# Transposing attention probabilities through the full TensorE array instead of through its halves

## The chip, the cores and the metric

The kernel runs on one core of one Trainium2 chip, as one program. The metric is the device time of one execution in microseconds. The core has a matrix engine (TensorE, PE in the profile, its weight loads PEld), VectorE (DVE), ScalarE (ACT), GpSimd (POOL) and SyncE (SP), which issues the DMA transfers. Each engine works through its own list of instructions in order; they meet through semaphores. All results of TensorE go to PSUM, which has eight banks here, each of 128 partitions by 512 numbers of 4 bytes.

## The reference

Two layers over a batch of 32 graphs of 512 nodes with 512 features, all in float32. The second layer is attention with 8 heads of 64 features, masked by the adjacency matrix:

```python
# layer 0
y = einsum('nm,bmd->bnd', adj, x)
x = layernorm(x + einsum('bnd,do->bno', y, weight) + bias)
# layer 1
qkv = (x @ w_qkv).reshape(b, n, 3, H, hd).transpose(2, 0, 3, 1, 4)
attn = einsum('bhnd,bhmd->bhnm', q, k) * hd ** -0.5
attn = where(adj == 0, -inf, attn)
attn = softmax(attn, axis=-1)
o = einsum('bhnm,bhmd->bhnd', attn, v).transpose(0, 2, 1, 3).reshape(b, n, d)
o = o @ w_proj + b_proj
out = layernorm(x + o + (layernorm of o with gamma and beta))
```

## The kernel before, in words

Every matrix product is made of three products of float32r operands: a number is split into a rounded part (hi) and the rest (lo), and hi*hi, hi*lo and lo*hi are added in PSUM. ScalarE makes the hi part by a copy, VectorE (for one tensor GpSimd) the lo part by a subtraction.

**The first layer** (0 to about 800 us) runs over the batch in rounds: `y` (line 332) and `z` (line 345) are matmuls over the full array, 128 rows by 512 columns. Between them, once a round, `turn_two` (line 221) transposes the previous result by halves of the array. Before the first round the adjacency is transposed once, by 16 transposes over the full array (line 152).

**The second layer** (the rest) goes through the batch `b`, and in each through 16 steps `k`: 4 pairs of heads (`group = k // 4`) by 4 blocks of 128 query rows (`k % 4`). A step has a chain that runs over all engines, spread over several steps:

- TensorE, `scores(b, k)` (line 819): scores of both heads of the pair for 128 query rows, 512 keys. One head has 64 features, so each matmul uses 64 rows of the array, and the two heads sit in its upper and lower half and run side by side, into two banks `s_bank`.
- VectorE, `masked_max` (line 1239), ScalarE, `exponent` (line 1119), VectorE, `inverse` (line 1248), GpSimd, `normalise` (lines 718 and 721): the softmax. The result is `probs[:, k % 2, a, :]`, for head `a`, with 128 query rows on the partitions.
- TensorE, `turn(k)` (line 835): transposes of `probs`, so that the keys come onto the partitions, into two banks `t_bank`. It signals `probs_turned`. In the profile this operation is named `bank<-ident,probs`: the probabilities are the weights, and the identity is what moves.
- ScalarE, `pt_hi_part` (line 1126), and VectorE, `pt_lo_part` (line 1259): the two parts of the transposed probabilities, out of `t_bank` into `pt_hi` and `pt_lo`. The views `turned` and `turned_into` say which part of a bank goes where.
- TensorE, `attend_v` (line 858): when the four query blocks of a pair are there, probabilities times values, again in two halves of the array (64 keys each).

Between these, TensorE is given filling work: the projections for values, queries and keys of the next batch, and the output projection (`half_pair`, lines 870 and 872, for the last batch also line 959). All of it is written as pairs of 64-row matmuls in the two halves of the array. The order on TensorE is written out by hand, in `first_step`, `second_step`, `third_step` and `last_step`: each begins with `turn(k)`, then come filling work or `attend_v`, then `scores` for step `k + 3`, and then the next turn. `ready_to_turn` holds TensorE before a turn until the probabilities are normalised and the lo part of the turn before has been taken from `t_bank`. The wait in `inverse` holds VectorE until a turn has read `probs`, because the next scores' maximum writes the same buffer.

SyncE loads and stores rows of whole batches and is not touched by the change.

Of the kernel before, what the change touches and what calls it, by code (L numbers as in the profile page):

```python
# [13 lines left out]
P = 128  # L14
# [4 lines left out]
def graph_layers(nc, x, adj, w0, b0, wqkv, wproj, bproj, gamma, beta, out):  # L19
    B, N, D = x.shape  # L20
    T = N // P
    HEAD = 64
# [16 lines left out]
    with ExitStack() as whole:  # L39
# [11 lines left out]
        ident = whole.enter_context(nc.sbuf_tensor("ident", [P, P], F32, side="right"))  # L51
# [21 lines left out]
        with ExitStack() as first:  # L73
            def sb(name, shape, dt):
                return first.enter_context(nc.sbuf_tensor(name, shape, dt))

            def sem(name):
                return whole.enter_context(nc.semaphore(name))
# [293 lines left out]
            def _(act):  # L372
# [33 lines left out]
                def batch(b, first=False, last=False):  # L406
                    for j in range(T):
                        y_hi_part(b, j)
                        w_hi_part(b, j)
                        if not first and j == 1:  # L410
                            for turned in range(T):
                                ut_hi_part(b - 1, turned)
                    if not last:
                        x_hi_part(b + 1)
                    if not first:
                        act.wait_ge(ub_made, b * 4)
                        act.wait_ge(u_turned, b * 4)
                    normalise(b, 0)
                    w_hi_part(b, 4)
                    normalise(b, 1)  # L420
                    w_hi_part(b, 5)
                    normalise(b, 2)
                    w_hi_part(b, 6)
                    normalise(b, 3)
                    w_hi_part(b, 7)
# [12 lines left out]
            def _(dve):  # L438
# [49 lines left out]
                def batch(b, first=False, last=False):  # L488
                    for j in range(T):
                        y_lo_part(b, j)  # L490
                        w_lo_part(b, j)
                        if not first and j == 1:
                            for turned in range(T):
                                ut_lo_part(b - 1, turned)
                    if not last:
                        x_lo_part(b + 1, 0)
                        x_lo_part(b + 1, 1)
                    row_stats(b, 0, free=not first)
                    if not last:
                        x_lo_part(b + 1, 2)  # L500
                    row_shift(b, 0)
                    row_stats(b, 1, free=not first)
                    if not last:
                        x_lo_part(b + 1, 3)
                    row_shift(b, 1)
                    w_lo_part(b, 4)
                    row_stats(b, 2)
                    row_shift(b, 2)
                    w_lo_part(b, 5)
                    row_stats(b, 3)  # L510
                    row_shift(b, 3)
                    w_lo_part(b, 6)
                    w_lo_part(b, 7)
# [13 lines left out]
        with ExitStack() as second:  # L527
# [11 lines left out]
            probs = sb("probs", [P, 2, 2, N], F32)  # L539
# [20 lines left out]
            s_bank, t_bank, o_bank = psum[0:2], psum[2:4], psum[4:6]  # L560
            g_bank = psum[6:8] + o_bank
            TOP, BOTTOM = slice(0, HEAD), slice(HEAD, P)
# [16 lines left out]
            probs_turned = sem("probs_turned")  # L579
# [41 lines left out]
            assert max(S_STEP) <= max(R_STEP) < 2 * STEPS  # L621

            def turned(i):
                return t_bank[i][:].rearrange("p (a m n) -> p a m n", a=2, m=T)

            def turned_into(rows, k, i):
                first = k % T * P + i * HEAD
                return rows[:, :, :, first:first + HEAD]

            def rows_of(b, n):  # L630

# [172 lines left out]
            def _(pe):  # L804
# [24 lines left out]
                def turn(k):  # L829

                    for a in range(2):
                        for m in range(T):
                            for i, h in enumerate((TOP, BOTTOM)):
                                cols = slice((a * T + m) * HEAD, (a * T + m + 1) * HEAD)
                                last = pe.transpose(t_bank[i][:, cols], probs[h, k % 2, a, m * P:(m + 1) * P],  # L835
                                                    ident[h, h])
                                if a == 1 and m == T - 1:
                                    last.then_inc(probs_turned, 1)

                def attend_v(b, p, part, run, half=None):  # L840

# [123 lines left out]
                def last_pair(b):  # L965

                    done = 4 * B - 4
                    turn(13)
                    pe.wait_ge(o_made, done)
                    pe.wait_ge(otlo_made, done + 2)  # L970
                    last_project(0, 0, (0, 1), first=True)
                    ready_to_turn(b, 14)
                    pe.wait_ge(proj_half, done + 2)
                    last_project(0, 1, (0, 1))
                    turn(14)

                    pe.wait_ge(ot_summed, b * 8 + 2 * LAST)
                    outputs(b, 0)
                    ready_to_turn(b, 15)
                    turn(15)  # L980
                    pe.wait_ge(otlo_made, done + 3)
                    last_project(0, 1, (2,))
# [132 lines left out]
            def _(act):  # L1115
# [5 lines left out]
                                       accum_out=sums[:, k % 4, a:a + 1]).then_inc(exp_made, 1)  # L1121

                def pt_hi_part(b, k):
                    act.wait_ge(probs_turned, b * 32 + (2 * k + 2))
                    for i in range(2):
                        act.activation(turned_into(pt_hi, k, i), turned(i), ACT.Copy).then_inc(pthi_made, 1)  # L1126

                def qk_hi_part(b, i):
# [52 lines left out]
                def batch(b, last_part=True, more=True):  # L1181
                    for k in range(STEPS):
                        group, part = divmod(k, T)
                        if part == 3 and group == 1:

                            ot_hi_part(b, 0)
                        if k == STEPS - 1 and not more:
                            last_ot_halves(0)
                        pt_hi_part(b, k)
                        if k == STEPS - 1 and not more:  # L1190
                            last_ot_hi(0)
                        if k + 2 < STEPS or more:
                            exponent(b, k + 2)
                        if part == 0 and (last_part or group > 0):
                            ot_halves(*pair_before(b, group))
                        if part in (1, 2):
                            unit_hi(b, k, 2 * part - 2, more)
                            unit_hi(b, k, 2 * part - 1, more)
                        if part == 1 and group != 1 and (last_part or group > 0):
                            ot_hi_part(*pair_before(b, group))  # L1200
                        for n in rows_at(k, Z_STEP) if last_part else ():
                            scaled(b, n)
                        for batch_row in rows_done(b, k, R_STEP, last_part):
                            result(*batch_row)
# [29 lines left out]
            def _(dve):  # L1234
# [18 lines left out]
                def pt_lo_part(b, k):  # L1253
                    if k % T == 0 and not (isinstance(b, int) and b * STEPS + k == 0):

                        dve.wait_ge(pv_done, b * 8 + k // 2)
                    for i in range(2):
                        dve.wait_ge(pthi_made, b * 32 + (2 * k + i + 1))
                        dve.tensor_tensor(turned_into(pt_lo, k, i), turned(i), f32(turned_into(pt_hi, k, i)),  # L1259
                                          ALU.subtract).then_inc(ptlo_made, 1)  # L1260
# [182 lines left out]
```

## Time and profile before

| | us |
|---|---|
| median of 3 runs | 3365.83 (3362.24 to 3365.88) |
| profiled execution, its own time | 3366.38 |
| its span in the trace | 3364.6 |
| TensorE busy, matmuls | 3308.5 (98%) |
| TensorE weight loads | 2923.1 (87%) |
| VectorE busy | 2623.7 (78%) |
| ScalarE busy | 2229.6 (66%) |
| GpSimd busy | 1997.1 (59%) |

The busy time of an engine is the time in which at least one of its instructions runs; matmuls overlap, since the end of one lies behind the start of the next, so the rate of TensorE is read from the distance between starts and not from durations. The transposes of line 835 are 8192 of TensorE's 31792 matmul records. The first layer is the part with heavy DMA traffic (168 to 195 GB/s in the slices that lie wholly in it), the second layer has 27 to 70 GB/s. The granted clock of TensorE is 1.0 or near it in all slices, with 0.8 in the first and the last.

### The profile page before, as it was taken

How to read it: one execution, taken by the hardware profiler on the slowest of the kernel's cores; microseconds unless marked ns; L12 is line 12 of the kernel's file. 1: busy time of each engine (PE TensorE's matmuls, PEld its weight loads, DVE VectorE, ACT ScalarE, POOL GpSimd, SP SyncE). 2: the span in 40 equal slices, each digit the busy share in tenths (PEclk: the TensorE clock that was granted, in tenths of full speed). 3: DMA queues.
4: the chain of work that ended last, by engine and by line, in shares of the span. 5: the costliest groups of instructions: out<-in, count | busy, mean ns of one | idle time of the engine just before them, and what ended most of it. 6: DMA issues, size and time to landing. Idle time of an engine off the chain costs nothing. (4 is left out here: it accounts for less than half of the span.)

```text
span 3364.6 us, 88016 instructions
## 1 busy us (share of the span) xinstructions
PE 3308.5 (98%) x31792; PEld 2923.1 (87%) x31792; DVE 2623.7 (78%) x6434; ACT 2229.6 (66%) x4634; POOL 1997.1 (59%) x2690
## 2 busy tenths in 40 slices
PE   8999999998999999999999999999999999999996
PEld 6888888886899998889899899899999899998894
DVE  7666666665788888888888888888888888888887
ACT  4444444444677777777777777777777777777775
POOL 4555556552466666666666666666666666666666
PEclk8999999998999999999999999999999999999998
DMA  5565555653011111111122211111111111111210
GB/s 188 174 195 168 186 187 172 190 180 102 27 52 51 55 54 51 51 55 51 51 63 66 66 51 51 51 51 51 51 54 54 51 51 54 51 51 53 70 59 32
DMA packets 345217, 279.62 MB, mean 83 GB/s; under 512 B 13713, under 2 KB 275857, under 8 KB 344977
## 3 DMA queue, kind: packets, MB, share of 16 engines
q1 hardware_dynamic: 344976, 275.83, 27.0%
q8 instruction: 222, 3.64, 0.5%
q14 instruction: 19, 0.15, 0.0%
HBM read 141.56 MB, written 134.22 MB: 82 GB/s over the span
## 5 line engine op out<-in xcount | busy, mean ns | idle before, releaser
L1126 ACT ACTIVATE pt_hi<-bank 128x512 fp32r<-128x512 f32 x1024 | 557.0, 596 | 546.3 <-PE bank L835 533.9
L1119 ACT ACTIVATE probs<-probs,bias_row 128x512 f32<-128x512 f32 x1024 | 731.7, 721 | 44.7 <-DVE bias_row L1239 43.6
L1259 DVE TENSOR_TENSOR pt_lo<-bank,pt_hi 128x512 fp32r<-128x512 f32 x1024 | 658.0, 684 | 44.0 <-PE bank L858 34.3
L721 POOL TENSOR_SCALAR probs<-probs,inv_sums 128x480 f32<-128x480 f32 (+1 forms) x1024 | 685.3, 682 | 0.0
L1239 DVE CUSTOM_DVE_ANT_0 probs<-bank,mask_bias 128x512 f32<-128x512 f32 x1024 | 661.9, 684 | 9.7 <-PE bank L819 5.8
L718 POOL TENSOR_TENSOR probs<-probs,inv_sums 128x32 f32<-128x32 f32 x512 | 122.7, 240 | 730.4 <-DVE inv_sums L1248 730.3
L872 PE MATMUL bank<-x_lo,w_hi 64*128 64x512 f32 x1024 | 403.3, 394 | 0.0
L870 PE MATMUL bank<-x_lo,w_hi 64*128 64x512 f32 x1024 | 403.3, 394 | 0.0
L872 PE MATMUL bank<-x_hi,w_hi 64*128 64x512 f32 x992 | 403.2, 406 | 0.0
L870 PE MATMUL bank<-x_hi,w_hi 64*128 64x512 f32 x992 | 401.6, 405 | 0.0
L835 PEld LDWEIGHTS bank<-ident,probs 64*128 64x128 f32 x8192 | 362.9, 139 | 40.8 <-issue 4.9
L870 PE MATMUL bank<-x_hi,w_lo 64*128 64x512 f32 x992 | 385.6, 389 | 0.0
L872 PE MATMUL bank<-x_hi,w_lo 64*128 64x512 f32 x992 | 385.3, 388 | 0.0
L835 PE MATMUL bank<-ident,probs 64*128 64x64 f32 x8192 | 350.6, 222 | 2.9 <-DVE pt_lo L1259 2.9
L1248 DVE RECIPROCAL inv_sums<-sums 128x2 f32<-128x2 f32 x512 | 84.0, 164 | 291.4 <-PE bank L835 287.5
L384 ACT ACTIVATE u<-res,shift,rstd 128x512 f32<-128x512 f32 x128 | 104.7, 818 | 307.0 <-DVE shift L467 307.0
L858 PE MATMUL bank<-pt_hi,v 64*128 64x512 f32 (+1 forms) x2064 | 299.3, 403 | 4.2 <-ACT pt_hi L1126 3.9
L858 PE MATMUL bank<-pt_lo,v 64*128 64x512 f32 (+1 forms) x2064 | 297.0, 399 | 0.4
L300 POOL TENSOR_TENSOR rstd<-var_eps,half_neg 128x1 f32<-128x1 f32 x128 | 95.8, 748 | 338.2 <-DVE var_eps L462 338.2
L761 POOL TENSOR_TENSOR ot_lo<-ot,ot_hi 128x512 fp32r<-128x512 f32 x127 | 164.5, 1295 | 209.3 <-ACT ot_hi L1161 209.3
L858 PEld LDWEIGHTS bank<-pt_hi,v 64*128 64x128 f32 x2064 | 208.3, 187 | 49.3 <-issue 32.1
L819 PE MATMUL bank<-k_hi,q_hi 64*128 64x512 f32 x1024 | 215.5, 390 | 8.0 <-DVE bias_row L1239 8.0
(139 smaller groups left out, 10847.2 us busy)
## 6 DMA issues: line engine op xcount, KB each, us to landing
x_in<-in_x_dram SPq DMA_DIRECT2D x32, 1024.0 KB, 5.2
u_beta_rows<-ub SPq DMA_DIRECT2D x32, 1024.0 KB, 4.4
ut_hi<-ut_hi_sb SPq DMA_DIRECT2D x128, 256.0 KB, 4.1
ut_lo<-ut_lo_sb SPq DMA_DIRECT2D x128, 256.0 KB, 3.8
x_lo<-ut_lo SPq DMA_DIRECT2D x128, 256.0 KB, 4.7
out_dram<-o SPq DMA_DIRECT2D x128, 256.0 KB, 3.2
ub_row<-u_beta_rows SPq DMA_DIRECT2D x124, 256.0 KB, 2.7
x_hi<-ut_hi SPq DMA_DIRECT2D x124, 256.0 KB, 4.4
```

Of the source, the lines that this page charges most:

```text
L718: pool.tensor_tensor(probs[:, k % 2, 0, strip], probs[:, k % 2, 0, strip], inv_sums[:, k % 4, 0:1].to_broadcast((P, STRIP)), ALU.mult)
L721: pool.tensor_scalar(probs[:, k % 2, a, cols], probs[:, k % 2, a, cols], inv_sums[:, k % 4, a:a + 1], 0.0, ALU.mult, ALU.add)\
L761: pool.tensor_tensor(ot_lo[:, p, :], ot[:], f32(ot_hi[:, p, :]), ALU.subtract)\
L819: last = pe.matmul(s_bank[a][:], l[h, pair, n * P:(n + 1) * P], r[h, pair, :], start=i == 0, stop=i == 2)
L835: last = pe.transpose(t_bank[i][:, cols], probs[h, k % 2, a, m * P:(m + 1) * P], ident[h, h])
L858: last = pe.matmul(bank[a][:, cols], w, part[h, a, m, cols], start=first and m == 0, stop=end and m == T - 1)
L870: top = pe.matmul(banks[run][:], left[run][TOP], right[run][TOP], start=run == 0 and first, stop=run == 1 and end)
L872: bottom = pe.matmul(banks[1 - run][:], left[1 - run][BOTTOM], right[1 - run][BOTTOM], start=run == 0 and first, stop=run == 1 and end)
L1119: act.activation(probs[:, k % 2, a, :], probs[:, k % 2, a, :], ACT.Exp, bias=bias_row[:, k % 4, a:a + 1], scale=-1.0, accum_out=sums[:, k ...
L1126: act.activation(turned_into(pt_hi, k, i), turned(i), ACT.Copy).then_inc(pthi_made, 1)
L1239: dve.tensor_tensor_reduce(probs[:, k % 2, a, :], s_bank[a][:], mask_bias[:, k % T, :], -SCALE, 3.0e38, ALU.add, ALU.min, bias_row[:, k % ...
L1259: dve.tensor_tensor(turned_into(pt_lo, k, i), turned(i), f32(turned_into(pt_hi, k, i)), ALU.subtract).then_inc(ptlo_made, 1)
```

## The change

`turn(k)` transposes 128 query rows by 128 keys at a time over the full array, with the whole identity, where it took 64 query rows by 128 keys in one half of the array and the other 64 rows in the other half. There are 8 transposes a step in place of 16. Before, bank `i` of `t_bank` held query rows `64 i` to `64 i + 63` of both heads; now bank `a` holds all 128 query rows of head `a`. `probs_turned` still rises by two a step, now once when head 0 is through and once when head 1 is. The views `turned` and `turned_into` follow the new layout, and ScalarE waits before each of its two copies for that head's signal, where it waited once for both. `pt_hi` and `pt_lo` hold the same numbers in the same places as before. Nothing else changes, and the order of the parts on each engine stays as it is.

```diff
             def turned(i):
-                return t_bank[i][:].rearrange("p (a m n) -> p a m n", a=2, m=T)
+                return t_bank[i][:].rearrange("p (m n) -> p m n", m=T)
 
             def turned_into(rows, k, i):
-                first = k % T * P + i * HEAD
-                return rows[:, :, :, first:first + HEAD]
+                return rows[:, i, :, k % T * P:(k % T + 1) * P]
...
                     for a in range(2):
                         for m in range(T):
-                            for i, h in enumerate((TOP, BOTTOM)):
-                                cols = slice((a * T + m) * HEAD, (a * T + m + 1) * HEAD)
-                                last = pe.transpose(t_bank[i][:, cols], probs[h, k % 2, a, m * P:(m + 1) * P],
-                                                    ident[h, h])
-                                if a == 1 and m == T - 1:
-                                    last.then_inc(probs_turned, 1)
+                            cols = slice(m * P, (m + 1) * P)
+                            last = pe.transpose(t_bank[a][:, cols], probs[:, k % 2, a, cols], ident[:])
+                            if m == T - 1:
+                                last.then_inc(probs_turned, 1)
...
                 def pt_hi_part(b, k):
-                    act.wait_ge(probs_turned, b * 32 + (2 * k + 2))
                     for i in range(2):
+                        act.wait_ge(probs_turned, b * 32 + (2 * k + i + 1))
                         act.activation(turned_into(pt_hi, k, i), turned(i), ACT.Copy).then_inc(pthi_made, 1)
```

## Rows read from the trace of the kernel before

**Rows 1.** The page's first part: busy us, share of span, instructions.
```profile
PE 3308.5 (98%) x31792; PEld 2923.1 (87%) x31792; DVE 2623.7 (78%) x6434; ACT 2229.6 (66%) x4634; POOL 1997.1 (59%) x2690
```

**Rows 2.** Stretches: length, busy PE, PEld, DVE, ACT, POOL, granted clock, DMA share, GB/s.
```profile
100.00:770.00 670.00, 667.86 (x3698) 548.50 (x3694) 444.08 (x924) 279.08 (x460) 374.12 (x345) 1.00 0.59 183
870.00:3200.00 2330.00, 2329.97 (x25396) 2117.67 (x25393) 1922.41 (x4926) 1748.92 (x3760) 1443.29 (x2110) 1.00 0.19 54
```

**Rows 3.** What TensorE waited for, whole run: total us, times, longest.
```profile
PE bank L819 <- DVE bias_row L1239: 8.0, 5, 2.1
...
PE bank L858 <- ACT pt_hi L1126: 3.9, 3, 1.3
...
PE bank L835 <- DVE pt_lo L1259: 2.9, 3, 1.0
```

**Rows 4.** TensorE in time order around one turn: start us, length us, instruction.
```profile
2002.84 0.42 PE L819 MATMUL bank<-k_hi,q_hi 64*128 64x512 f32 x2
...
2003.29 0.42 PE L819 MATMUL bank<-k_hi,q_lo 64*128 64x512 f32 x2
2003.53 0.68 PE L835 MATMUL bank<-ident,probs 64*128 64x64 f32 x16
2003.99 0.47 PE L870 MATMUL bank<-w_hi,ot_hi 64*128 64x512 f32 x1
...
2004.31 0.38 PE L870 MATMUL bank<-w_lo,ot_hi 64*128 64x512 f32 x1
```

**Rows 5.** Line 835: the page's group; then weight loads in attention, min/median/max ns.
```profile
L835 PE MATMUL bank<-ident,probs 64*128 64x64 f32 x8192 | 350.6, 222 | 2.9 <-DVE pt_lo L1259 2.9
...
L835 PEld LDWEIGHTS bank<-ident,probs x7957: 134/139/221, 869.9 to 3333.0; 64*128 64x128 f32 x199
```

**Rows 6.** Full-array transposes of line 152: durations, and single ones in time order.
```profile
L152 PEld LDWEIGHTS bank<-ident,u x16: 141/230/231, 3.5 to 6.9; 128*128 128x128 f32 x16
L152 PE MATMUL bank<-ident,u x16: 273/421/476, 3.5 to 7.0; 128*128 128x128 f32 x16
...
4.61 0.63 PE L152 MATMUL bank<-ident,u 128*128 128x128 f32 x2
...
6.94 0.38 PE L152 MATMUL bank<-ident,u 128*128 128x128 f32 x2
...
7.05 0.27 PE L152 MATMUL bank<-ident,u 128*128 128x128 f32 x1
```

**Rows 7.** Busy time and granted clock (third number from the end) in the first stretches.
```profile
3.00:5.00 2.00, 1.49 (x7) 1.52 (x8) 0.85 (x2) 0.00 (x0) 0.00 (x0) 1.00 0.93 274
...
12.00:16.00 4.00, 3.31 (x8) 2.64 (x9) 4.00 (x5) 2.72 (x6) 2.79 (x2) 0.50 1.12 343
18.00:24.00 6.00, 6.00 (x28) 4.92 (x28) 4.89 (x7) 2.77 (x6) 1.84 (x2) 1.00 0.60 195
```

**Rows 8.** Full-array matmuls of 512 columns at both clocks, in time order.
```profile
14.56 1.91 PE L332 MATMUL bank<-adjt_lo,x_hi 128*128 128x512 f32 x4
...
21.25 1.07 PE L332 MATMUL bank<-adjt_lo,x_hi 128*128 128x512 f32 x4
```

**Rows 9.** Half-array transposes between full-array matmuls, first layer; matmuls, then weight loads.
```profile
422.95 0.39 PE L332 MATMUL bank<-adjt_hi,x_lo 128*128 128x512 f32 x1
423.27 1.21 PE L221 MATMUL bank<-ident,u 64*128 64x64 f32 x32
424.41 0.50 PE L332 MATMUL bank<-adjt_hi,x_hi 128*128 128x512 f32 x1
...
424.74 0.40 PE L332 MATMUL bank<-adjt_hi,x_hi 128*128 128x512 f32 x1
...
423.27 1.07 PEld L221 LDWEIGHTS bank<-ident,u 64*128 64x128 f32 x32 [0.35 <-issue]
```

**Rows 10.** The page's costliest groups: ScalarE's copy and VectorE's subtraction of the transposed probabilities.
```profile
L1126 ACT ACTIVATE pt_hi<-bank 128x512 fp32r<-128x512 f32 x1024 | 557.0, 596 | 546.3 <-PE bank L835 533.9
...
L1259 DVE TENSOR_TENSOR pt_lo<-bank,pt_hi 128x512 fp32r<-128x512 f32 x1024 | 658.0, 684 | 44.0 <-PE bank L858 34.3
```

## The prediction, made before the changed kernel ran

> **What bounds the kernel now.** I read the busy times first, then a table of the stretches, then who waited for whom, then the order of time around one step. TensorE is busy for 98% of the span [rows 1]. In the long stretch of attention, 870 to 3200 us, it is busy for 2329.97 of 2330 us at a granted clock of 1.00, while VectorE has 1922, ScalarE 1749 and GpSimd 1443 us [rows 2]. Busy alone could hide stalls, so the waits: on the lines of attention TensorE waited for another engine 8.0, 3.9 and 2.9 us in the whole run (lines 819, 858 and 835), 14.8 us together [rows 3]. The two halves of the array run side by side, and the start of one pair of 64-row matmuls comes 0.23 us after the start of the pair before (2002.84 and 2003.29, with one more pair between them) [rows 4]. So the end is set by how long the TensorE stream is, and a change of the transposes is worth what it does to that stream, nearly one to one. The ScalarE waits for transposes and the idle time of VectorE and GpSimd cost nothing now.
>
> **What a turn costs before.** There are 512 turns (32 batches of 16 steps), 8192 transposes [rows 5]. The last score pair starts at 2003.29, so it is through its slot at 2003.52; the turn starts at 2003.53 and the next work starts at 2003.99; but that first pair is long (0.47 where others take 0.39) and the second one starts at 2004.31, 0.32 later, not 0.23 [rows 4]. From slot end to the regular rhythm again: 2004.31 - 0.23 - 2003.52 = **0.56 us** a turn. Of this the transposes are 16 in two streams: 0.68 less one duration of 0.22 over 15 intervals is 0.031 us each, 0.061 a pair, 0.49 for eight pairs; 0.07 is the way back to matmuls with long weights.
>
> **What a turn costs after.** Removed: 16 transposes of 64 rows by 64 moving columns, two at a time. Added: 8 transposes of 128 rows by 128 moving columns, one at a time. Work by columns: before 8 pairs of 64, after 8 of 128, so if a column costs the same, the streaming doubles.
>
> The trace of before has this very operation, on the adjacency at the start (line 152, 128*128 by 128x128, the same data type): the last two start at 6.94 and 7.05, **0.11 us** apart, and last 0.27 us, the smallest duration [rows 6]. The earlier ones last 0.42 and are 0.21 apart (two that start at 4.61 are through after 0.63) [rows 6]. Which is the one to use? The granted clock is recorded as 1.00 from 3 to 5 us and as 0.50 from 12 to 16 us [rows 7], but the factor of two with the same shape is that between the two levels of the clock: the 128x512 matmuls of line 332 take 1.91 us for four at 14.56, where 0.50 was granted, and 1.07 at 21.25, with 1.00 [rows 7, 8]. I take 0.11, the only value that fits the full level, and keep 0.21 as the upper end. The lower end is 0.061, the interval of a pair of half-array transposes, if the load of the 128 weight columns and not the moving columns sets it: 8 x 0.11 = 0.88 (0.49 to 1.68).
>
> **The change between halves and full array.** All else in attention is 64-row work, so each turn now goes over to the full array and back. That also is in the trace, with the parts exchanged: in the first layer 32 half-array transposes stand between full-array matmuls. The last full matmul before starts at 422.95, its slot of 0.23 ends at 423.18; the transposes start only at 423.27; the first full matmul after starts at 424.41, takes 0.50 in place of 0.39, and the second follows at 424.74 [rows 9]. From slot end to rhythm: 424.74 - 0.23 - 423.18 = 1.33 us. Sixteen pairs at 0.061 are 0.98, so the round trip costs **0.35 us**: 0.09 in which TensorE stands before the transposes, about 0.05 for a first weight load with nothing over it, 0.09 and 0.11 for the same on the way back. The weight loads show it too: an idle time of 0.35 us ended by issue, where otherwise a load runs under each matmul [rows 9]. The Trainium skill, TensorEngine Tiling (Array Packing), Key Properties, says that changing the tiling mode drains TensorE, which the gap before 423.27 agrees with.
>
> A turn after is thus 0.88 + 0.35 = 1.23 us, against 0.56. The 0.07 of the way back before is replaced by the round trip's own. **Difference 0.67 us x 512 = +343 us.**
>
> **What hides or gives back.** Nothing lies over it: TensorE is the engine with no gaps. The way of a step that runs beside it (turn done, reciprocal and scores' maximum, the low part, next turn) starts from the end of a turn and has the same TensorE work as before to run under, so it isn't late now. The waits that exist (14.8 us) can shrink, since ScalarE gets its first tile when four transposes are through and no longer after all 16, and the long weights' exposure adds room; I take 4 us back of them. The new wait on ScalarE, one for each tile, sits ahead of the copies of line 1126, where ScalarE waits for TensorE already (533.9 us of idle time in all), so what is queued behind it (exponents, values' copies) comes no later relative to the end of the turn. The copies of 1126 and the subtractions of 1259 now read and write blocks of 128 and not 64 elements; 512 elements a row as before, at 596 and 684 ns [rows 10]; if each changed by a tenth, it would be in the shade of TensorE. The queue of SyncE is untouched. The last turn starts at 3333.0 [rows 5], so the last 32 us, where the layer norms of the last rows end the program, have none.
>
> Sum against the profiled execution: 3366.4 us (its span 3364.6), + 343 - 4 = 3705. The median of the runs shown is 3365.83, the same within 0.02%. **Forecast 3705 us**, +10%.
>
> **Rivals.**
> - The way there and back costs nothing here, because the neighbours are 64-row matmuls, whose drain might lie under the other half. For: nothing in rows 4 shows such a cost when transposes follow matmuls in one mode. Against: rows 9 at both edges, in the same form in all later rounds of the first layer. Turn 0.88 + 0.07 = 0.95, +0.39 x 512 = +200: 3566 us.
> - The moving columns of a full transpose are not the limit, the weight load is (0.061 each). For: a weight load of 64 rows and one of 128 rows take the same (139 ns, the median of line 835, and 141 ns, the smallest of line 152) [rows 5, 6], so eight loads in place of sixteen would be no more work. Against: the 0.11 at 6.94 to 7.05. Turn 0.49 + 0.35 = 0.84, +143: 3509 us. The skill's TensorE page (TensorE: Matmul & The Clock Gate, Back-to-back issue gap) gives some 81 ns for a sustained pair of load and 128-column matmul; by it the turn would be 1.00 us and the time about 3590. The row disagrees with 81 ns, and is for this data type; the chance of this rival covers that value too.
> - **Faster, the other side**: the transposes are bound by their number, 0.031 us for each issued whatever its size. Then eight cost 0.25, and with no cost of changing over the turn is 0.32: -0.24 x 512 = -123, 3243 us. This is what would make the edit a gain. It decides at (0.56 - change-over) / 8: a full transpose would have to take under 0.06 us with a free change-over, under 0.03 with the one measured. Against it stands again the 0.11.
> - TensorE falls to its lower clock level in places, because it now stands still twice in each step and spends more on transposes. If one step in ten ran at half clock, attention (about 2840 us after) would add some 280: near 3990 us. For: in a stretch in which TensorE was busy 3.31 of 4.00 us, 0.50 was granted [rows 7]. Against: 100 to 770 us, with such round trips, has 1.00 throughout [rows 2]. The skill's section PE-mode transpose says that transposes do not count as busy for the clock in the way matmuls do; the stretch with 32 of them in each round does not show a fall.
> - 0.21 us a full transpose at full clock: turn 2.03, +753: 4119 us.
>
> **How the numbers follow.** Forecast 0.84; free change-over 0.05; weight-load bound 0.04; faster by number of instructions 0.02; fallen clock 0.03; 0.21 us each 0.01; 0.01 for something that leaves the time alone. The range needs only the forecast's own uncertainty: the interval of a full transpose is read at 0.01 us (0.105 to 0.115 is 0.04 a turn, 20 us in all), the round trip may differ from 0.35 by 0.05 with halves as neighbours (26 us), the waits by 10 us: 3650 to 3755. A measurement of this kernel tells about 0.2% (7 us) from no change: faster 0.02, same 0.01, slower 0.97.
>
> **What will show it.** In the profile after: 4096 transposes of 128*128 128x128, median 0.27 us long, starting 0.11 apart (the main term; at 0.06 the second rival holds); the first one some 0.09 us later than the slot end of the last score pair, and the pair after the turn long, about 0.50 (else the first rival); 1.23 us from slot end to rhythm; granted clock 1.00 in the long stretch; TensorE still without waits in it, VectorE and ScalarE at lower shares and busy for the same microseconds. The forecast is wrong if TensorE waits appear on 819, 835 or 858, since I take the loop through the other engines as unchanged.

## The result and the profile after

The changed kernel takes 3681.32 us (median of 4 runs, 3679.2 to 3684.78) against 3365.68 us; the ratio is 1.094, with a 95% interval of 1.0926 to 1.0958. It is 316 us slower; forecast were 339.

The first part of the page, as [rows 1], and then the stretch of attention, as [rows 2] (stretch, length, busy time of PE, PEld, DVE, ACT and POOL, granted clock, DMA share, GB/s):

```profile
PE 3628.7 (99%) x27696; PEld 2860.8 (78%) x27696; DVE 2624.2 (71%) x6434; ACT 2263.7 (61%) x4634; POOL 2001.0 (54%) x2690
```

```profile
870.00:3500.00 2630.00, 2630.00 (x21666) 2056.30 (x21664) 1927.54 (x4934) 1782.99 (x3768) 1448.54 (x2111) 1.00 0.16 48
```

VectorE and GpSimd are busy for the same microseconds as in [rows 1], to within 4 us, ScalarE for 34 us more, which costs nothing, since it waits for TensorE anyway; TensorE is busy 320 us longer with 4096 fewer matmuls, without a gap in the long stretch, and at full granted clock. So the whole difference lies in TensorE's stream. Here is one turn of it, TensorE in order of time as in [rows 4], then its weight loads:

```profile
2200.86 0.39 PE L818 MATMUL bank<-k_lo,q_hi 64*128 64x512 f32 x2
2201.08 0.39 PE L818 MATMUL bank<-k_hi,q_lo 64*128 64x512 f32 x2
2201.40 1.09 PE L833 MATMUL bank<-ident,probs 128*128 128x128 f32 x8
2202.43 0.50 PE L867 MATMUL bank<-x_hi,w_hi 64*128 64x512 f32 x1
...
2202.76 0.39 PE L867 MATMUL bank<-x_lo,w_hi 64*128 64x512 f32 x1
...
2201.40 0.86 PEld L833 LDWEIGHTS bank<-ident,probs 128*128 128x128 f32 x8 [0.35 <-issue]
2202.42 0.18 PEld L867 LDWEIGHTS bank<-x_hi,w_hi 64*128 64x128 f32 x1 [0.17 <-issue]
```

The slot of the last score pair ends at 2201.08 + 0.23 = 2201.31 and the rhythm is regular again at 2202.76 - 0.23 = 2202.53: 1.22 us, where [rows 4] gave 0.56. From the start of one of the eight transposes to the start of the next it is 0.165 us for the first and 0.109 for the other six, in the mean of the turns of batches 1 to 29: the 0.11 of [rows 6], and about 0.06 for the first weight load, which has nothing to run under. The 0.09 us before 2201.40, the long first pair of 0.50 after it and the weight loads that had to wait for the other mode (0.35 and 0.17) are those of [rows 9] with the parts exchanged. All steps together, the page's group, and the durations in attention (min/median/max ns):

```profile
L833 PE MATMUL bank<-ident,probs 128*128 128x128 f32 x4096 | 562.5, 281 | 2.8 <-DVE pt_lo L1256 2.8
```

```profile
L833 PE MATMUL bank<-ident,probs x3984: 272/273/472, 872.3 to 3648.0; 128*128 128x128 f32 x200
```

### The profile page after: what moved, and what is told of

It is laid out like the page before. It is cut to its first block and busy times, and to the rows that moved or that the text cites. A ratio compares the mean times of both kernels' runs of the same rounds, so it can differ in the third digit from the quotient of the medians.

```text
span 3682.9 us, 79882 instructions
## 1 busy us (share of the span) xinstructions
PE 3628.7 (99%) x27696; PEld 2860.8 (78%) x27696; DVE 2624.2 (71%) x6434; ACT 2263.7 (61%) x4634; POOL 2001.0 (54%) x2690
## 5 line engine op out<-in xcount | busy, mean ns | idle before, releaser
L833 PEld LDWEIGHTS bank<-ident,probs 128*128 128x128 f32 x4096 | 440.9, 141 | 170.5 <-issue 170.4
L833 PE MATMUL bank<-ident,probs 128*128 128x128 f32 x4096 | 562.5, 281 | 2.8 <-DVE pt_lo L1256 2.8
L855 PE MATMUL bank<-pt_hi,v 64*128 64x512 f32 (+1 forms) x2064 | 279.5, 389 | 2.8 <-ACT pt_hi L1123 2.4
L867 PEld LDWEIGHTS bank<-x_hi,w_hi 64*128 64x128 f32 x992 | 182.8, 184 | 65.5 <-issue 30.8
L855 PEld LDWEIGHTS bank<-pt_hi,v 64*128 64x128 f32 x2064 | 193.4, 185 | 47.9 <-PE bank L855 2.4
```

Source lines behind the costliest of these rows:

```text
L833: last = pe.transpose(t_bank[a][:, cols], probs[:, k % 2, a, cols], ident[:])
L855: last = pe.matmul(bank[a][:, cols], w, part[h, a, m, cols], start=first and m == 0, stop=end and m == T - 1)
L867: top = pe.matmul(banks[run][:], left[run][TOP], right[run][TOP], start=run == 0 and first, stop=run == 1 and end)
```

## The experiments

### What one transpose and one change-over cost

Three runs. **Half of the full-array transposes** (e3):

```diff
                             cols = slice(m * P, (m + 1) * P)
-                            last = pe.transpose(t_bank[a][:, cols], probs[:, k % 2, a, cols], ident[:])
+                            if m % 2 == 0:
+                                last = pe.transpose(t_bank[a][:, cols], probs[:, k % 2, a, cols], ident[:])
```

> The changed kernel with only every second of its full-array transposes (4 of 8 a step; the other key blocks of the transposed probabilities are left out, so the outputs are other numbers). If each transpose costs 0.109 us and the rest of the turn is fixed, the turn falls from 1.225 to 0.79 us and the time to 3681 - 512 x 0.436 = 3458 us. If a transpose were really 0.061 us and the change-over larger, it falls by 125 us only, to 3556 us.

Measured: 3466.46 us, one run, 215 us below the changed kernel.

```profile
2009.59 0.39 PE L818 MATMUL bank<-k_hi,q_lo 64*128 64x512 f32 x2
2009.91 0.66 PE L834 MATMUL bank<-ident,probs 128*128 128x128 f32 x4
2010.50 0.49 PE L868 MATMUL bank<-x_hi,w_hi 64*128 64x512 f32 x1
...
2010.83 0.39 PE L868 MATMUL bank<-x_lo,w_hi 64*128 64x512 f32 x1
```

The turn is 2010.83 - 0.23 - 2009.82 = 0.78 us, 0.44 less for four transposes less: 0.11 each. What is left without any transpose is 1.22 - 8 x 0.11 = 0.34, the change-over. The 215 us are 0.42 a turn, 10 us in all short of 0.44.

**Fewer weight columns** (e8):

```diff
-                            last = pe.transpose(t_bank[a][:, cols], probs[:, k % 2, a, cols], ident[:])
+                            last = pe.transpose(t_bank[a][0:HEAD, cols], probs[:, k % 2, a, m * P:m * P + HEAD],
+                                                ident[:])
```

> The changed kernel with transposes of 64 keys in place of 128: 64 weight columns, still 128 rows and 128 moving columns (the other 64 keys of each block are left out, so the outputs are other numbers). If the moving columns set the 0.109 us between starts, the turn stays 1.22 us and the time 3681 us (within 15 us); if the weight load sets them, the interval falls to about 0.055 us and the time to about 3460 us.

Measured: 3671.68 us, one run.

```profile
2013.16 1.06 PE L833 MATMUL bank<-ident,probs 128*64 128x128 f32 x8
2014.16 0.49 PE L868 MATMUL bank<-x_hi,w_hi 64*128 64x512 f32 x1
```

With weights half as wide the eight transposes still take 1.06 us from first start to last end, 0.03 less and not half: the six later intervals stay at 0.109 us, and only the first, with nothing over its load, falls, from 0.165 to 0.136. So the width of the weights does not set the 0.11 us, and the rival of the weight load falls. The moving columns are what is left: 64 of them take 0.061 us in half-array pairs and 128 take 0.109 here; no run varied them alone. The rival of a cost by number falls too, since a full transpose takes 0.109 and not 0.031.

**The change-over alone** (e2): the kernel before, its half-array transposes kept, with one small full-array matmul ahead of each turn.

```diff
                 def turn(k):
 
+                    pe.matmul(t_bank[0][:, 0:64], w_hi[:, 0, 0, 0:P], w_hi[:, 0, 0, 0:64], start=True, stop=True)
                     for a in range(2):
```

> The kernel before, half-array transposes, with one small full-array matmul (weights from w_hi, 64 moving columns, written into a bank that the turn then overwrites) put ahead of each turn. It measures the round trip between halves and full array with the transposes unchanged. Forecast: the turn grows from 0.555 by the round trip of 0.35 us and about 0.03 to 0.06 for the matmul, 512 x 0.39 = +200 us, about 3565 us; if the change-over costs nothing +15 to +30 us, about 3390 us. Theory R keeps the late pt_hi in the last steps (pairs there 258 and 309 ns apart); rival S expects the halves 3 ns apart and the time some 15 to 20 us lower than the sum, as in the changed kernel.

Measured: 3557.78 us (3555.07 to 3559.53), ratio 1.0574 [1.0556, 1.0592], +192 us.

```profile
2011.99 0.40 PE L819 MATMUL bank<-k_hi,q_lo 64*128 64x512 f32 x2
2012.32 0.30 PE L831 MATMUL bank<-w_hi 128*128 128x64 f32 x1
2012.55 0.71 PE L836 MATMUL bank<-ident,probs 64*128 64x64 f32 x16
2013.07 0.71 PE L859 MATMUL bank<-pt_lo,v 64*128 64x512 f32 x4
```

A matmul that leaves nothing behind costs 192/512 = 0.375 us a turn: the score pair's slot ends at 2012.22, the small matmul starts at 2012.32, and the half-array transposes 0.23 after it. That fits the forecast's 0.35 and the 0.03 to 0.06 that was put down for the matmul itself; the free change-over is out. The Trainium skill, TensorEngine Tiling (Array Packing), Key Properties, states that a change of tiling mode drains TensorE. The trace agrees, with 0.10 us in which nothing starts before 2012.32, and this run prices two changes, with halves as neighbours.

### Where 23 us of the forecast went

The turn costs what was forecast, and yet the kernel loses less than 512 x 0.67. I compared the distances between the starts of matmul pairs step by step. In the kernel before, the first use of `pt_hi` in each last step comes late. TensorE and its weight loads, kernel before, then the changed one:

```profile
2005.22 0.39 PE L870 MATMUL bank<-w_hi,ot_lo 64*128 64x512 f32 x1
...
2005.48 0.50 PE L858 MATMUL bank<-pt_hi,v 64*128 64x512 f32 x2
...
2005.45 0.79 PEld L858 LDWEIGHTS bank<-pt_hi,v 64*128 64x128 f32 x8 [0.23 <-issue]
```

```profile
2203.69 0.39 PE L867 MATMUL bank<-x_hi,w_lo 64*128 64x512 f32 x1
...
2203.92 0.39 PE L855 MATMUL bank<-pt_hi,v 64*128 64x512 f32 x2
...
2203.69 0.87 PEld L855 LDWEIGHTS bank<-pt_hi,v 64*128 64x128 f32 x8
```

Before, the weight load waits 0.23 us, and the matmul is delayed 0.11 us in all over its first two intervals (0.258 and 0.309 us in the mean of 118 last steps, where 0.227 is regular). But the record of a delayed matmul begins before its weights are there, so TensorE counts as busy and the list of waits [rows 3] stays nearly empty. Grouped by line it shows in the weight loads, whole run, kernel before, then changed kernel:

```profile
L858 PEld LDWEIGHTS bank<-pt_hi,v 64*128 64x128 f32 x2064 | 208.3, 187 | 49.3 <-issue 32.1 <-PE bank L858 2.4 <-DVE v L1270 1.4
```

```profile
L855 PEld LDWEIGHTS bank<-pt_hi,v 64*128 64x128 f32 x2064 | 193.4, 185 | 47.9 <-PE bank L855 2.4 <-issue 2.4 <-DVE v L1267 1.0
```

Two explanations: ScalarE starts on head 0 earlier now (theory R), or the two halves of the array run less skewed after a full-array stretch and this makes the pairs follow each other faster (rival S): the two matmuls of a pair start 3 ns apart in the changed kernel, and 27 ns (scores) to some 90 ns (filling work) in the mean before. **One signal** (e1) undoes the first in the changed kernel:

```diff
                 def pt_hi_part(b, k):
+                    act.wait_ge(probs_turned, b * 32 + (2 * k + 2))
                     for i in range(2):
-                        act.wait_ge(probs_turned, b * 32 + (2 * k + i + 1))
```

> The changed kernel with one edit undone: ScalarE waits once, for both heads' signals, before its two copies, as before the change; the transposes stay over the full array. Theory R (the 24 us by which the change cost less than forecast come from ScalarE's earlier start on head 0: TensorE waited some 0.12 us in each last step for pt_hi and some 0.07 us in each first step before the next turn, unseen in the list of waits): the waits come back, the turn stays 1.22 us, and the time is 3681 + 128 x 0.19 = about 3705 us, ratio to before 1.101. Rival S (the two halves start 3 ns apart after each full-array stretch in place of 30 ns, and this makes the pairs denser): time stays 3681 us, ratio 1.094.

Measured: 3685.27 us, ratio 1.0952 [1.0934, 1.097]; 4 us and not 24 came back, and 4 us lie within the interval, so **theory R falls**. S does not explain the late first use either, by e2: there the halves start 3 ns apart in the first pair after every turn, and that use is as late as before:

```profile
L859 PEld LDWEIGHTS bank<-pt_hi,v 64*128 64x128 f32 x2064 | 208.4, 185 | 49.6 <-issue 34.3 <-PE bank L859 2.4 <-DVE v L1271 1.4
```

What e2 lacks and both kernels with full-array transposes have is a change-over, and so standing time, *between* a turn and the matmuls behind it. ScalarE's copies in a last step, kernel before, changed kernel, and e1:

```profile
2004.25 1.09 ACT L1126 ACTIVATE pt_hi<-bank 128x512 fp32r<-128x512 f32 x2
```

```profile
2202.09 1.09 ACT L1123 ACTIVATE pt_hi<-bank 128x512 fp32r<-128x512 f32 x2
```

```profile
2022.24 1.09 ACT L1123 ACTIVATE pt_hi<-bank 128x512 fp32r<-128x512 f32 x2 [0.59 <-PE bank L833]
```

From the start of the turn: before, `pt_hi` is done at 2005.34 - 2003.53 = 1.81 us and TensorE could load its weights at 2005.22 - 2003.53 = 1.69, too early. Changed, it is done at 2203.18 - 2201.40 = 1.78, and TensorE comes for it at 2203.69 - 2201.40 = 2.29. With one signal the copies end at 2023.33 and the turn started at 2021.11, 2.22, and the weight load comes for them at 2.33 in the mean of the last steps: still in time. The longer turn itself, with 0.20 us of standing behind it, covers the wait. **Theory T**: part of the new cost was paid with standing time that was there already.

A second such place is the turn after each first step. TensorE and VectorE, kernel before:

```profile
2032.73 0.39 PE L870 MATMUL bank<-x_hi,w_lo 64*128 64x512 f32 x1
...
2033.05 0.47 PE L870 MATMUL bank<-x_hi,w_hi 64*128 64x512 f32 x1
...
2033.35 0.34 PE L835 MATMUL bank<-ident,probs 64*128 64x64 f32 x5
...
2031.61 1.29 DVE L1259 TENSOR_TENSOR pt_lo<-bank,pt_hi 128x512 fp32r<-128x512 f32 x2
```

`ready_to_turn` stands one piece of filling work ahead of the turn; the low part ends at 2032.90, and that piece starts at 2033.05, 0.32 after the one before, not 0.23, and the turn again 0.07 late. In the mean of the first steps the two are late by 0.04 and 0.06 us.

T says that the waits can be covered in other ways, and that this helps the kernel before and not the changed one. **Eight pieces** (e4 in the kernel before, e10 in the changed one):

```diff
                         if more_fill:
-                            fill(group + 1, 0, 6)
+                            fill(group + 1, 0, 8)
...
                         attend_v(b, group, pt_hi, 0)
-                        if more_fill:
-                            fill(group + 1, 6, 2)
+                        scores_ahead(k)
                         attend_v(b, group, pt_hi, 1)
-                        scores_ahead(k, turn_next=True)
+                        if k + 1 < STEPS or more:
+                            ready_to_turn(b + (k + 1) // STEPS, (k + 1) % STEPS)
```

> The kernel before, half-array transposes, with another order in the last step of each pair of heads: all eight pieces of filling work before the first part of attend_v, and the scores between its two parts (before: six pieces, first part, two pieces, second part, scores). Theory T (part of the change's cost was paid by standing time that was there before: in each last step TensorE waited about 0.12 us for pt_hi, seen as two intervals of 258 and 309 ns in place of 227, and the 0.2 us of the way back from the full array now lie over it): with the wait taken away otherwise, this kernel gains 128 x 0.11 = 14 us, 3351 us, ratio 0.996. If that wait is not real idle time (a matter of how the halves are skewed), 3365 us.

Measured: 3350.89 us, ratio 0.9958 [0.9945, 0.9972], as expected.

```profile
L858 PEld LDWEIGHTS bank<-pt_hi,v 64*128 64x128 f32 x2064 | 221.7, 185 | 18.4 <-issue 2.8 <-DVE v L1270 1.4 <-PE bank L858 0.6
```

> The same other order in the changed kernel. Theory T: the wait for pt_hi is already covered by the way back from the full array, so nothing is left to gain, 3681 us (within 4 us); the difference between this kernel and the one with half-array transposes and the same order is then the full 0.67 us a turn, 330 to 340 us. If the order brings 14 us by other means than that wait, 3667 us.

Measured: 3677.22 us, ratio 1.0926 [1.0911, 1.0941]. 4 us of gain, the edge of what T allowed, where the kernel before got 14. The gap to e4 is 326 us, less than the 330 to 340 written down: the second place is still open.

**Seven and one** (e5): the calls become `fill(group + 1, 0, 7)` and `fill(group + 1, 7, 1)`, the rest as before.

> The kernel before with seven pieces of filling work before the first part of attend_v and one between the parts, in place of six and two. Theory T: the wait for pt_hi of 0.12 us goes, as with eight (14 us, 3351 us), unless the second part then waits for the first one's results: with one piece between, 0.227 us, against a matmul's record of 0.39 us from start to end, a wait of up to 0.15 us would take its place and the time would be 3365 us or above.

Measured: 3367.92 us, ratio 1.0009 [0.9999, 1.0018]. The branch with the new wait: at the first use the intervals are regular, and the second part of `attend_v`, with one piece ahead of it, now begins with intervals of 0.254 and 0.335 us. The wait moved by one place.

**Statistics later** (e9b), on the second place:

```diff
+                        pt_lo_part(b, k)
                         if part == 0:
                             rows_statistics(b, k, last_part)
-                        pt_lo_part(b, k)
```

> The kernel before with one reordering on VectorE: in the first step of each pair of heads the statistics of the output rows come after the low part of the transposed probabilities, not ahead of it. It tests the second place where the change cost less than forecast: the turn after a first step starts up to 0.08 us late before, beside an interval of 262 ns, and ready_to_turn waits there for the low part. If that lateness is a wait for VectorE, 128 x 0.05 to 0.1 = 6 to 12 us are gained, about 3357 us; if it is TensorE's own, the time stays 3365 us.

Measured: 3442.9 us, ratio 1.0231 [1.0217, 1.0245], **78 us slower**, which neither side expected. The turn after a first step did come earlier: the interval ahead of it is 0.227 us in place of 0.262 in the mean, and the turn's own 0.273 in place of 0.295, so the wait was for the larger part VectorE's. But in the second step the scores now wait, by this row of the list of waits, where [rows 3] had 8.0:

```profile
PE bank L819 <- DVE bias_row L1239: 64.3, 95, 3.2
```

The mean interval ahead of the second step's scores is 0.825 us where it was 0.227, and the next one is 0.06 too long: 0.66 us, 84 us over 128 second steps, less some 7 us gained ahead of the turns. The trace shows where it comes from. The low part of a first step waits for `attend_v` (line 858) to be through with `pt_lo`, and before, the statistics ran in that time. VectorE in one first step, kernel before (its turn started at 1988.72), then e9b (turn at 2024.67):

```profile
1990.78 0.69 DVE L1293 BATCH_NORM_STATS2 o_stats<-o 128x6 f32<-128x512 f32 x1
...
1991.98 1.29 DVE L1259 TENSOR_TENSOR pt_lo<-bank,pt_hi 128x512 fp32r<-128x512 f32 x2
...
1994.82 0.69 DVE L1239 CUSTOM_DVE_ANT_0 probs<-bank,mask_bias 128x512 f32<-128x512 f32 x1
```

```profile
2027.88 1.29 DVE L1259 TENSOR_TENSOR pt_lo<-bank,pt_hi 128x512 fp32r<-128x512 f32 x2 [1.09 <-PE bank L858]
2029.09 0.69 DVE L1293 BATCH_NORM_STATS2 o_stats<-o 128x6 f32<-128x512 f32 x1
...
2031.84 0.69 DVE L1239 CUSTOM_DVE_ANT_0 probs<-bank,mask_bias 128x512 f32<-128x512 f32 x1
```

VectorE's waits for line 858 ahead of the low part grow from 34.3 to 128.4 us. The low part starts 3.21 us after the turn in place of 3.26, hardly earlier, but 1.1 us of statistics now stand behind it, and the next scores' maximum starts 7.17 us after the turn in place of 6.10. One of the four first steps of a batch has no statistics; its second step stays at 5.80 us in the mean, while the other three grow to 6.71: 96 x 0.91 = 87 us, less the gain ahead of the turns.

**One more piece** (e11 and e12) covers the second place by work on TensorE, together with the order of e4:

```diff
-                        fill_and_wait(group, 12, 4, k + 1)
+                        fill_and_wait(group, 12, 5, k + 1)
...
-                            fill(group, 16, 10)
+                            fill(group, 17, 9)
```

> The kernel before, half-array transposes, with both standing times of TensorE covered by work: the last step's order of the run before last (eight pieces of filling work, first part of attend_v, scores, second part), and one piece of filling work (0.227 us) moved from the second step to the first, ahead of the turn that stood up to 0.15 us waiting for the low part. Theory T: 3351 - 128 x 0.12 = 3336 us, ratio 0.991; faster than both kernels. If the lateness of that turn is TensorE's own, 3351 us.

Measured: 3339.31 us, ratio **0.9925** [0.9912, 0.9939]. Faster than both kernels; 3 us above what was written.

> The same two moves in the changed kernel, transposes over the full array. Theory T: in the changed kernel only some 0.05 us a group are left of the second standing time, so it gains about 6 us on 3677: 3671 us. The difference to the same order with half-array transposes is then the full price of the transposes, 512 x (1.225 - 0.555) = 343 us less some 5 us at the ends, 335 us (330 to 345). If the change also saved time by some other means that these moves don't touch, the difference stays near 326 us or below.

Measured: 3670.35 us, ratio 1.0907 [1.0892, 1.0922]. The two kernels of this pair, alike but for the transposes, are 331 us apart, 0.65 us a turn, inside the 330 to 345 written down, at its lower edge.

## Why the prediction was right

Measured 3681, forecast 3705, range 3650 to 3755.

- **TensorE bounds, nothing lies over the turn.** Right in the main: its stream shows no gap in attention in either kernel, and e11 with e12 show almost the whole price once the old waits are covered otherwise. But the prediction also held that the way through the other engines "isn't late now"; at two places in each group it was late by some 0.1 us, and the longer turn lay over that.
- **A full transpose 0.11 us.** Right, 0.109 in the changed kernel and by difference in e3; e8 shows that the width of the weights does not set it. The choice of 0.11 over 0.21 [rows 6] rested on the two clock levels and held.
- **Change-over 0.35 us.** Right: 0.34 by e3, and e2 paid 0.375 with the small matmul. The forecast's parts are there too, in the mean of the turns: 0.09 standing before the first transpose, 0.06 for the first load, 0.09 and 0.11 on the way back.
- **Difference 0.67 us a turn.** Right in the trace (1.22 against 0.56).
- **What gives back: 4 us.** This is the term that was mis-sized; it was 343 - 316 = 27 us. The prediction took the 14.8 us of [rows 3] for all of TensorE's waits. The short waits at the first use of `pt_hi` and at the low part, some 0.1 us each, are hidden in that view. By their times, e4 recovers 14 us in the kernel before and e10 4 us in the changed one, e11 another 12 and e12 another 7: about 15 of the 27 us (the two kernels' distance grows from 316 to 331 us, each with an interval of some 5 us) are waits that the longer turn covered. Of the other 12, some 6 us are in the last batch, where TensorE waits in any case: from the batch's first turn to the end e11 takes 105.0 us, with TensorE busy for 74.9 of them, and e12 109.8, not 16 x 0.67 = 10.7 more. The rest lies in the pairs behind the turn. In third steps, where no pair waits, a turn starts 3.995 us after the one before in the kernel before and 4.647 in the changed one, 0.65 more and not 0.67: less the turn itself, 3.44 us are left before and 3.42 after. The skew of the halves is not the reason, since e3 and e8 have the same 3 ns and 3.44 us; what is, stays open.
- **The reason given for it**, ScalarE's earlier start, was the wrong one: e1 puts it at 4 us. It was the standing time behind the turn.
- The clock stayed at 1.00 in the long stretch, and no wait was added on the lines named: 818, 833 and 855 have 7.2, 2.8 and 2.4 us for the causes of [rows 3], which had 8.0, 2.9 and 3.9, and one new wait of 0.6 us stands on 818.

## What to carry to other kernels

Before work is moved between halves of the array and the full array, look for the same operation elsewhere in the trace: the price of one transpose and of one change-over stood in the first layer of this kernel, and the sum came out to 0.7% of the time. Count moving columns and not instructions: here eight transposes of 128 columns one at a time cost 0.88 us where sixteen of 64 in two streams cost 0.49. And where an engine counts as busy all the time, look at the distance between starts against the regular one, and at the weight loads' idle time, for waits that the list of waits doesn't show; covering two of them here by the order of the work gave 0.75%.

## What I had not expected of the hardware

A matmul whose weights wait for another engine is recorded from before they are there (0.50 for two at 2005.48, where 0.39 to 0.42 is usual), so waits of 0.1 us leave the busy share at 100%; what shows them are the distances between starts and, of the grouped views, the 32.1 us of idle weight loads ended by "issue". Narrower weights (64 columns, tile 128*64) changed the interval of transposes by nothing. And a reordering on VectorE that took some 0.06 us off a wait cost 78 us in all, since it put 1.1 us of work behind a wait that it had filled before.
